# The order of the tail of a fused attention and expert-layer kernel: q's and o's low parts, the last z's and one buffer

## What is computed

```
x = x + attention(layernorm(x), ctx)      # 32 query heads, 8 key/value heads of 16, rotary positions, softmax, Wo
x = x + experts(layernorm(x))             # 64 experts of rank 8, the best 16 per token
```

## Time and profile before

| what | value |
|---|---|
| median of three runs | 184.85 us (184.71 to 184.86) |
| the profiled execution's own time | 184.47 us |
| its span in the profile | 182.5 us |
| TensorE busy | 169.6 us, 93% of the span |
| DVE busy | 133.0 us, 73% |
| ACT busy | 90.0 us, 49% |
| POOL busy | 85.6 us, 47% |
| chain that ended last, by engine | PE 57%, POOL 18%, DVE 10%, issue 10% |

### The profile page before, as it was taken

The page is one execution under the profiler, slowest core; times in us unless marked ns, Lnnn a source line. Parts: engine busy times, 40 slices in busy tenths (PEclk is TensorE's granted clock), DMA queues, the critical chain, the costliest instruction groups (busy, mean ns, idle before and its releaser), DMA issues.

```text
span 182.5 us, 4057 instructions
## 1 busy us (share of the span) xinstructions
PE 169.6 (93%) x1440; PEld 130.9 (72%) x1440; DVE 133.0 (73%) x391; ACT 90.0 (49%) x206; POOL 85.6 (47%) x109
## 2 busy tenths in 40 slices
PE   7999999988969999999999999999997999599874
PEld 2656575666749887888788878978695767499653
DVE  2667858978994999569954997569938969465461
ACT  3579899636456534742665274644272360432210
POOL 5599989599488349131840275035503020603000
PEclk9999999999999999999999999999999999999999
DMA  5999802001101010101010000100010001000111
GB/s 180 300 400 392 348 4 59 2 12 49 61 3 54 4 57 0 63 0 57 5 57 0 4 0 0 63 0 0 4 57 0 4 0 57 4 4 0 57 57 58
DMA packets 5331, 11.30 MB, mean 62 GB/s; under 512 B 688, under 2 KB 944, under 8 KB 5056
## 3 DMA queue, kind: packets, MB, share of 16 engines
q1 hardware_dynamic: 5024, 10.79, 16.7%
q10 hardware_dynamic: 288, 0.27, 0.4%
HBM read 8.95 MB, written 2.10 MB: 61 GB/s over the span
## 4 chain that ended last, share of the span: by engine, by line
PE 57%; POOL 18%; DVE 10%; issue 10%; DMA 2%; ACT 1%; DVEq 0%; POOLq 0%
PE ps_w L1039 10%; PE ps_w L1044 10%; PE ps_w L1040 9%; PE ps_t L1052 6%; PE ps_s L1099 5%; POOL am_lo L268 3%; PE ps_s L1135 3%; PE ps_s L1118 3%; POOL wo_lo L268 3%; POOL wq_lo L268 2%; PE ps_w L1032 2%; PE ps_w L1033 2%; PE ps_w L1034 2%; POOL k_bd_hi L301 2%; POOL k_bd_lo L301 2%
## 5 line engine op out<-in xcount | busy, mean ns | idle before, releaser
L325 POOL TENSOR_TENSOR late<-late,gate 128x512 f32<-128x512 f32 x7 | 7.6, 1081 | 45.0 <-DVE gate L854 39.3
L310 POOL TENSOR_TENSOR oT_lo<-o_n,oT_hi 128x512 fp32r<-128x512 f32 x8 | 10.3, 1285 | 29.2 <-ACT oT_hi L505 29.2
L761 DVE TENSOR_REDUCE ps_s<-ps_s 128x8 f32<-128x512 f32 x32 | 20.8, 693 | 1.0 <-PE ps_s L1099 0.7
L497 ACT ACTIVATE eT<-ps_s 128x512 f32<-128x512 f32 x32 | 17.0, 598 | 4.1 <-PE ps_s L1124 4.0
L1039 PE MATMUL ps_w<-b_hi,zT_hi 128*128 128x512 f32 (+1 forms) x32 | 12.8, 405 | 1.6 <-ACT zT_hi L545 1.6
L1039 PE MATMUL ps_w<-am_hi,x2T_hi 128*128 128x288 f32 x48 | 13.9, 311 | 0.0
L1040 PE MATMUL ps_w<-am_lo,x2T_hi 128*128 128x288 f32 x48 | 13.1, 296 | 0.0
L505 ACT ACTIVATE oT_hi<-o_n 128x512 fp32r<-128x512 f32 x8 | 5.1, 634 | 14.4 <-DVE o_n L794 14.4
L1040 PE MATMUL ps_w<-b_lo,zT_hi 128*128 128x512 f32 (+1 forms) x32 | 12.1, 381 | 0.0
L1039 PE MATMUL ps_w<-wo_hi,oT_hi 128*128 128x512 f32 x28 | 11.7, 419 | 0.4 <-ACT oT_hi L505 0.4
L1200 PE MATMUL ps_w<-wq_sb,xT_raw 128*128 128x512 f32 x24 | 11.8, 606 | 0.0
(11 more groups left out here) (203 smaller groups left out, 526.4 us busy)
## 6 DMA issues: line engine op xcount, KB each, us to landing
x_sb<-x SPq DMA_DIRECT2D x8, 256.0 KB, 7.2
cT_in<-cT SPq DMA_DIRECT2D x7, 256.0 KB, 2.7
out<-res SPq DMA_DIRECT2D x7, 256.0 KB, 2.0
wq_sb<-wq SPq DMA_DIRECT2D x4, 256.0 KB, 6.4
late<-wo SPq DMA_DIRECT2D x1, 1024.0 KB, 8.3
am_sb<-aT SPq DMA_DIRECT2D x1, 1024.0 KB, 8.5
b_sb<-bT SPq DMA_DIRECT2D x1, 1024.0 KB, 7.1
wkv_sb<-wkv SPq DMA_DIRECT2D x1, 512.0 KB, 4.9
```

Of the source, the lines that this page charges most:

```text
L310: pool.tensor_tensor(oT_lo[:], o_n[:].rearrange("p (b r q) -> p r b q", b=2, r=REP), oT_hi[:].bitcast(F32), ALU.subtract).then_inc(oT_lo_o ...
L497: act.activation(eT[:, c].rearrange("p b n -> p (b n)"), ps_s[:, c, :], ACT.Exp)\
L761: dve.tensor_reduce(neg_top[:, b, HALF_H * half:HALF_H * (half + 1), :], ps_s[:, 2 * (1 - b) + half, :].rearrange("p (r h k) -> p h r k", ...
```

## The change

It reorders the lists of the tail and moves one tile's turned z to another buffer:
- ACT: `q_high(l)` stands one exponential earlier, `expert_exps(a)` ahead of the exponentials of tile l and not behind them, `z_high(a)` behind `expert_scores(m)` and `z_first(m)`.
- DVE: `q_low(l)` stands within `route(z)`; `route(a)` is moved from behind `attend(m)` into its `meanwhile`; `z_low(a)` comes behind `route(m)`, `z_low(m)` within `route(l)`; `gated_last` is ahead of `result(a)`, `z_low(l)` ahead of `result(m)`.
- POOL: `o_low(l)` is ahead of `gated(a)`, `deviation2(l)` ahead of `gated(m)`.
- TensorE: `up_high(z)` is spread otherwise around `turn_m` and `turned_scores`; `out_high(l)` is ahead of `turn_x2(m)`, `turn_zg(a)` behind `project_down(m, 0)`, `turn_zg(m)` ahead of the up product of a, `turn_zg(l)` between the two parts of that of m.
- The turned z of tile m (T - 2) goes to `xT_hi` and `xT_lo`. `z_high(m)` waits for the last down product there, and `z_high(l)` for the up product of a.

```diff
--- before.py
+++ after.py
@@ -156,6 +156,9 @@
 
         def x2T_of(t):
             return (x2T_hi, x2T_lo) if t < T - 1 else (xT_hi, xT_lo)
+
+        def zT_of(t):
+            return (xT_hi, xT_lo) if t == T - 2 else (zT_hi, zT_lo)
 
         def x2T_bank(t):
             return ps_t0 if t == T - 1 else ps_t1
@@ -408,11 +411,11 @@
                 gated(z)
                 deviation2(a)
                 o_low(m)
+                o_low(l)
                 gated(a)
                 deviation2(m)
-                o_low(l)
+                deviation2(l)
                 gated(m)
-                deviation2(l)
 
             first()
             second()
@@ -540,9 +543,11 @@
 
             def z_high(t):
                 act.wait_ge(zT_ps, t + 1)
-                if t >= 1:
-                    act.wait_ge(up_ps, t)
-                act.activation(zT_hi[:], ps_t1[:].rearrange("p (k q) -> p k q", k=DK), ACT.Copy)\
+                if t == T - 2:
+                    act.wait_ge(z_ps, 2 * T)
+                elif t >= 1:
+                    act.wait_ge(up_ps, min(t, T - 2))
+                act.activation(zT_of(t)[0][:], ps_t1[:].rearrange("p (k q) -> p k q", k=DK), ACT.Copy)\
                    .then_inc(zT_hi_ok, 1)
 
             def x_raw(t):
@@ -649,9 +654,9 @@
                 for c in range(PAIRS - 1):
                     exps(m, c)
                 expert_scores(z)
+                q_high(l)
                 exps(m, PAIRS - 1)
                 z_first(z)
-                q_high(l)
                 expert_exps(z)
                 z_second(z)
                 x2_high(a)
@@ -659,17 +664,17 @@
                 expert_scores(a)
                 z_first(a)
                 m_out(l)
+                expert_exps(a)
                 for c in range(PAIRS):
                     exps(l, c)
-                expert_exps(a)
                 o_high(m)
                 o_high(l)
                 x2_centre(m)
                 z_second(a)
                 x2_high(m)
-                z_high(a)
                 expert_scores(m)
                 z_first(m)
+                z_high(a)
                 x2_high(l)
                 expert_exps(m)
                 z_second(m)
@@ -880,9 +885,10 @@
                 dve.tensor_scalar_add(x2_c[:], x2_of(t), x2_mean[:]).then_inc(x2_c_ok, 1)
 
             def z_low(t):
+                hi, lo = zT_of(t)
                 dve.wait_ge(zT_hi_ok, t + 1)
-                dve.tensor_tensor(zT_lo[:], ps_t1[:].rearrange("p (k q) -> p k q", k=DK),
-                                  zT_hi[:].bitcast(F32), ALU.subtract).then_inc(zT_lo_ok, 1)
+                dve.tensor_tensor(lo[:], ps_t1[:].rearrange("p (k q) -> p k q", k=DK),
+                                  hi[:].bitcast(F32), ALU.subtract).then_inc(zT_lo_ok, 1)
 
             def result(t):
                 dve.wait_ge(up_ps, t + 1)
@@ -995,12 +1001,11 @@
                     top(l, 1)
                     m_parts(l)
                     z_low(z)
-
-                route(z)
+                    route(a)
+
+                route(z, lambda: q_low(l))
                 x2_low(a)
-                q_low(l)
                 attend(m, maxima)
-                route(a)
                 result(z)
                 attend(l)
                 residual(m)
@@ -1009,14 +1014,13 @@
                 residual(l)
                 x2_centre_last()
                 statistics2(l)
+                route(m, lambda: x2_low(l))
                 z_low(a)
-                route(m, lambda: x2_low(l))
+                route(l, lambda: z_low(m))
+                gated_last()
                 result(a)
-                route(l)
-                z_low(m)
-                gated_last()
+                z_low(l)
                 result(m)
-                z_low(l)
                 result_last()
 
             first()
@@ -1178,11 +1182,11 @@
                 if t == 0:
                     pe.wait_ge(b_l, DK)
                 pe.wait_ge(zT_hi_ok, t + 1)
-                high_part(up_of(t), chunk(zT_hi), b_hi, b_lo, slice(0, D), chunks)
+                high_part(up_of(t), chunk(zT_of(t)[0]), b_hi, b_lo, slice(0, D), chunks)
 
             def up_low(t):
                 pe.wait_ge(zT_lo_ok, t + 1)
-                low_part(up_of(t), chunk(zT_lo), b_hi, slice(0, D)).then_inc(up_ps, 1)
+                low_part(up_of(t), chunk(zT_of(t)[1]), b_hi, slice(0, D)).then_inc(up_ps, 1)
 
             def raw_kv(t):
                 pe.wait_ge(ld_c[t], 16)
@@ -1319,24 +1323,26 @@
                 scores(l, 1)
                 pe.wait_ge(z_ok, 2 * z + 1)
                 project_down(a, 0)
+                pe.wait_ge(z_ok, 2 * z + 2)
+                up_high(z, [0])
                 pe.wait_ge(qT_lo_ok, T)
                 turn_m(l)
-                pe.wait_ge(z_ok, 2 * z + 2)
-                up_high(z, [0])
+                up_high(z, [1])
                 turned_scores(l)
-                up_high(z, [1, 2, 3])
+                up_high(z, [2, 3])
                 up_low(z)
                 values(l)
                 pe.wait_ge(z_ok, 2 * a + 1)
                 project_out(m)
                 project_down(a, 1)
+                out_high(l)
                 pe.wait_ge(zT_lo_ok, z + 1)
                 turn_x2(m)
-                project_out(l)
+                out_low(l)
+                pe.wait_ge(x2_ok, l)
+                project_down(m, 0)
                 pe.wait_ge(x2T_lo_ok, m + 1)
                 turn_zg(a)
-                pe.wait_ge(x2_ok, l)
-                project_down(m, 0)
                 pe.wait_ge(mT_ok, T)
                 turn_x2(l)
                 pe.wait_ge(z_ok, 2 * a + 2)
@@ -1344,16 +1350,16 @@
                 pe.wait_ge(o_step, 3 * T - 2)
                 project_down(l, 0)
                 project_down(l, 1)
+                pe.wait_ge(zT_lo_ok, a + 1)
+                turn_zg(m)
                 pe.wait_ge(res_ok, z + 1)
                 up_high(a)
                 up_low(a)
-                pe.wait_ge(zT_lo_ok, a + 1)
-                turn_zg(m)
+                pe.wait_ge(zT_lo_ok, m + 1)
                 pe.wait_ge(z_ok, 2 * m + 1)
                 up_high(m)
+                turn_zg(l)
                 up_low(m)
-                pe.wait_ge(zT_lo_ok, m + 1)
-                turn_zg(l)
                 pe.wait_ge(res_ok, a + 1)
                 pe.wait_ge(x2T_lo_ok, T)
                 pe.wait_ge(zT_hi_ok, T)
```

## The result

The changed kernel takes 178.97 us (median of four, 178.29 to 180.68) against 184.78 beside it: a ratio of 0.9706, 95% interval 0.9647 to 0.9764. The forecast was 179.3 in a range of 178.6 to 181.0. The profiled execution took 179.04 us, 5.43 less than that of before.

The account below looks back on a forecast made before the run. TensorE was taken to bound the tail, with some 5 us of holes from other engines' order. Rebuilding its queue put the last up product 5.5 us earlier: 184.47 - 5.5 = 178.97 profiled, 184.85 - 5.5 = 179.3 median; range 178.6 to 181.0.

Parts of the forecast that it names:

- the pause for x_c(7): TensorE ahead of turn_x2(7), waiting for residual(7) behind x2_low(6): a new pause of 0.34 us.
- that for zg(6): TensorE ahead of turn_zg(6), which now comes before up(5): a pause of 0.3 us, until 164.8.
- the upper bound of 2.93: DVE's route(6) with x2_low(7) inside: at most 2.93 us, at least 2.33 if the low part fits into waits.
- Output products: Stretch up to out_low(7): out_high(6) 0.98 us earlier, then out_low(7) done by 157.0, a gain of 3.5.
- gate(5) at 0.25 and not at 1.11: DVE step in route(5): 0.25 us since POOL is idle then; a rival with chance 0.12 had 0.86 more, 180.2.
- The price is covered by values(7), with nothing to spare: route(5) before attend(6)'s tail delays o_n(6), yet oT_hi(6) is ready at 149.1, just as TensorE finishes values(7).
- The end: Stretch from route(6) on: last up product at 171.3, 5.5 us earlier, with gated_last 1.0 ahead of turn_zg(7).
- The pauses of 0.33 and of twice 0.78: TensorE waits around up_high(6), its low part and the last up product: covered by up(5) and up_low(6), so gone.
- the rival in which the end isn't closed: POOL's gated(6) or route(7) over 1.0 us late, old pauses return: 1.9 us more, 181.2; chance 0.08.
- the slower one: Rival behind down(7,1): late zg(6) delays turn_zg(6) and up(5) one for one, giving 186.9; chance 0.02.
- the piece of 5.70 us called issue: Piece in the chain of waits before its last 24 us, put on DVE; expected to be absent after the change.
- The rival by which the buffer does nothing because the order alone gives it: z of tile 6 in the x buffer changes nothing in the time; chance 0.01.

Follow-up runs that it names:

- u_route_free: Changed kernel with route(5) back behind attend(6), its exponential behind tile 7's, and POOL's oT_lo(6) made to wait for gate(5): 179.65 us, tail +0.32.
- u_route: Changed kernel with route(5) back behind attend(6) on DVE and its exponential behind those of tile 7 on ACT: 179.57 us, tail +1.18.
- a_gate: Changed kernel with gated(6) ahead of deviation2(7) on POOL, as before the change: 178.41 us, tail -0.22.
- u_buf: Changed kernel with the turned z of tile 6 in the z buffer again, all orders kept: 181.17 us, tail +2.82.
- u_turn: Changed kernel with turn_zg(7) behind up_low(6) again, not between the parts of up(6): 179.58 us, tail +0.92.
- p_busy: Changed kernel with one more POOL instruction, an unread 128x512 subtraction meant to run over gate(5): 179.36 us, tail +0.97.
- o_buf: Kernel before with only the buffer edit, turned z of tile 6 in the x buffer: 184.76 us, tail 39.07 against 39.04.
- u_pool: Changed kernel with POOL's o_low(7) again behind gated(5) and deviation2(6): 179.83 us, tail +1.23.

## Why the prediction was right

*The timetable.* Taking the 0.67 of the later start off, the measured starts stand beside the forecast ones so:

| start of | forecast | measured - 0.67 |
|---|---|---|
| scores(7,0) | directly behind values(6) | 138.79 (values(6) + 1.02) |
| values(7) | 148.1 | 147.94 |
| out_high(6) | 149.1 | 149.00 |
| down(5,1) | 152.0 | 151.88 |
| out_high(7) | 153.6 | 153.48 |
| turn_x2(6) | 155.57 | 155.35 |
| turn_x2(7) | 159.3 | 159.02 |
| turn_zg(6) | 164.8 | 164.49 |
| up_high(6) | 168.0 | 167.75 |
| last up product | 171.3 | 170.99 |

The gain of the tail was forecast as 5.5 and is 5.82. The 0.3 comes in small pieces, nearly all one way. out_high(7) behind a down product costs 1.87 (154.15 to 156.02), not the 1.97 of a product behind the small matmuls of values; the pause for x_c(7) is 0.25, not 0.34; that for zg(6) 0.22, not 0.3; and values(7) was 0.16 early. That is 0.43; two stretches were some 0.06 longer than forecast, from values(7) to out_high(6) (1.06, not 1.0) and from turn_zg(6) to up_high(6) (3.26, not 3.2). That the profiled execution took 179.04 us, beside the 178.97 of the prediction's sum for it, is partly luck: the 0.3 gained in the tail, and 0.2 less outside the span, make up for the 0.67 by which the tail began later. route(6) with x2_low(7) inside takes 2.81 (160.48 to 163.03 + 0.26), near the upper bound of 2.93.

*Output products.* The step that was decided against the bare row, gate(5) at 0.25 and not at 1.11, held. Taken as a fixed cost it would have been 0.86 more, and u_route_free and u_route differ by just that. "The price is covered by values(7), with nothing to spare" held as well: oT_hi(6) ends at 149.52 and out_high(6) starts at 149.67.

*The end.* Ahead of turn_zg(7) the forecast had 1.0 us to spare; gated_last ends at 169.16, turn_zg(7) starts at 170.28. The pauses of 0.33 and of twice 0.78 are gone, and only the 0.22 ahead of turn_zg(6) came in their place, so the rival in which the end isn't closed and the slower one fell.

*Where a step was off.* Of what the profile of the changed kernel would show, one item was wrong: oT_lo(7) starts 1.25 ahead of gated(5), not "about 2 us". The timetable of the same prediction had it right, with POOL's queue doing one directly behind the other. The first reading of the chain was off as well: it put the piece of 5.70 us called issue on DVE. The piece ends where POOL's gated(5) starts and is as long as POOL's idle time ahead of it, 5.71 in the earlier trace rows, and what gated(5) waited for was ACT's z_second(5), as the prediction itself says further on. The sum doesn't use it. From values(6) on, the chain of the changed kernel has no piece called issue over 0.2 us. The prediction also took deviation2(7) ahead of gated(6) as given and charged its 0.5 us to the pause of zg(6) without weighing the old order; a_gate shows that this part of the change costs 0.22. The rival by which the buffer does nothing because the order alone gives it was false: with the order kept and the buffer undone, 2.82 of the 5.82 are lost (u_buf).

*Adding up.* The parts don't simply add. Four of them undone singly cost 1.23 + 1.18 + 2.82 + 0.83 = 6.06, and with u_turn's 0.92 it is 6.98, against 5.82 for all at once. A part of that is counted twice: in u_buf the last copy of z lies open as in u_turn (its pause of 0.84, beside u_turn's 0.78). The rest isn't taken apart, and the new places of turn_zg(6) and out_high(7) on TensorE weren't undone alone.

## What to carry to other kernels

Where one engine is the bound and runs a list in order, write its queue out with start-to-start durations and, at each wait, the moment its input comes; that gave the worth of nine edits here to within 0.2 us (of the tenth, p_busy, it named the wrong victim), where the pauses in the profile named the wrong size (0.65 for 1.23) or the wrong step. The second buffer was worth something only where the order asked for the data early (2.82 us, and nothing in o_buf), so try the two together. And before moving a step of DVE, look at what POOL reads at that time, as gate, a quarter-us instruction that met it, took 1.11 us.

## What the runs showed of the hardware that was not expected

- *DVE and POOL stall each other also early in the kernel.* Of DVE's instructions at L788, 0.42 us each as a rule, the first of the first tile took 1.57 (the two together 1.90). It started at 30.51, behind POOL's second am_lo instruction (30.38 to 31.80), and ended at 32.08, 0.28 behind it. The other way round, POOL's k_bd_lo took 1.49 us at 14.41, where it takes 1.04 otherwise: DVE's q_r, with two SBUF inputs, had started at 14.02 and ran to 15.00. Rows of the kernel before:

```profile
30.51 1.90 DVE L788 TENSOR_TENSOR o_t<-o_s,inv 128x256 f32<-128x256 f32 x2
...
29.01 2.79 POOL L268 TENSOR_TENSOR am_lo<-am_sb,am_hi 128x576 fp32r<-128x576 f32 x2
...
14.02 0.98 DVE L939 TENSOR_TENSOR q_r<-q_a,q_b 128x512 f32<-128x512 f32 x1
...
14.41 1.49 POOL L301 TENSOR_TENSOR k_bd_lo<-kT_lo,half_mask 128x512 fp32r<-128x512 f32 x1
```

Both are in the changed kernel too (1.90 and 1.49), and it was not tried to remove them, so that these two are such stalls is read from the overlap alone.
- *The start varies.* values(6) began between 137.66 (u_pool) and 138.44 us (the changed kernel) in executions whose programs do the same up to there but for small moves on ACT and DVE just ahead of it. Before and after the change, attend(0) already starts at 28.83 and at 29.49, so the difference comes from the first 29 us, in which the first loads arrive (the chain gives the first load of x 4% of the span after the change). What in them varies stays open.
